# Layer 0 of a two-layer kernel rebuilt: two expert slots instead of three experts, one block, activation split on VectorE

## The reference

```python
xn = _layernorm(x, axis=-1)
s = _L0_attn_ref(xn, Wq, bq, Wk, bk, Wv, bv)      # per token: q, k, v of 16 x heads; 16 x 16 scores, softmax, mix
g = _silu(_L0_ffn_ref(xn, gate_w, gate_b, w1, b1, w2, b2))
x = x + s * g
...
# in _L0_ffn_ref
router_input = jnp.concatenate([h, modality_ratio], axis=-1)
gate_scores = jax.nn.softmax(router_input @ gate_w + gate_b, axis=-1)
top_val, top_idx = jax.lax.top_k(gate_scores, TOP_K)              # TOP_K = 2 of 3
top_val = top_val / (jnp.sum(top_val, axis=-1, keepdims=True) + 1e-08)
expert_out = _expert_outputs(h, w1, b1, w2, b2)                   # tanh, gelu, silu
for i in range(TOP_K):
    j = top_idx[:, 0, i]                                          # the expert of the batch's FIRST token
    moe_out = moe_out + top_val[..., i:i + 1] * expert_out[j, batch_idx]
```

## Time and profile before

| what | value |
|---|---|
| median of the runs | 1755.26 us |
| the profiled execution's own time | 1760.71 us |
| its span | 1759.0 us |
| TensorE busy | 1498.3 us (85%), mean granted clock 0.914 |
| VectorE busy | 1146.7 us (65%) |
| ScalarE busy | 604.9 us |
| GpSimd busy | 340.3 us |
| first product with an expert's matrix starts | 88.29 us |
| last operation of layer 0 on VectorE ends | 521.1 us |

### The profile page before, as it was taken

How to read it: one execution, slowest core, us unless ns; L and a number is a source line. 1 busy time by engine, 2 the same in 40 slices (tenths; PEclk the granted TensorE clock), 3 DMA queues, 4 the chain that set the end, 5 groups by cost and what they waited for, 6 DMA issues and landing times. The chain is left out here.

```text
span 1759.0 us, 21810 instructions
## 1 busy us (share of the span) xinstructions
PE 1498.3 (85%) x7034; PEld 1025.7 (58%) x7034; DVE 1146.7 (65%) x2429; ACT 604.9 (34%) x859; POOL 340.3 (19%) x382
## 2 busy tenths in 40 slices
PE   0399979898855884799999999599999999999969
PEld 0366757576634552577777777455555555555447
DVE  5575875858754544555555544388888888888427
ACT  4223233232312431011111111016666666666632
POOL 2243342433411320000000000002122221221211
PEclk9988988889876987799999999759999999999979
DMA  7200010100004433000000000221221211211032
GB/s 258 105 1 1 0 49 0 48 1 1 24 26 151 161 123 114 31 22 27 25 19 19 22 11 4 48 42 28 42 43 28 55 29 29 55 29 29 1 133 83
DMA packets 48600, 84.27 MB, mean 48 GB/s; under 512 B 8899, under 2 KB 16657, under 8 KB 48506
## 3 DMA queue, kind: packets, MB, share of 16 engines
q1 hardware_dynamic: 41874, 78.13, 15.1%
q10 hardware_dynamic: 6632, 4.97, 0.9%
HBM read 58.54 MB, written 24.26 MB: 47 GB/s over the span
## 5 line engine op out<-in xcount | busy, mean ns | idle before, releaser
L1502 ACT ACTIVATE f_prob<-f_bank 128x1024 f32<-128x1024 f32 (+3 forms) x384 | 302.1, 811 | 187.7 <-PE f_bank L1599 183.9
L1522 DVE CUSTOM_DVE_ANT_0 f_bank<-f_bank,f_mask 128x128 f32<-128x128 f32 (+3 forms) x512 | 247.7, 504 | 67.4 <-PE f_bank L1581 54.6
L1581 PE MATMUL f_bank<-f_kst,f_qst 96*128 96x512 f32 (+3 forms) x768 | 271.1, 398 | 14.3 <-DMA f_qst<-q_scr 12.2
L1581 PEld LDWEIGHTS f_bank<-f_kst,f_qst 96*128 96x128 f32 x768 | 148.3, 197 | 161.5 <-DVE f_mx L1522 58.0
L1599 PE MATMUL f_bank<-f_qst,f_kst 98*128 98x512 f32 (+3 forms) x768 | 210.3, 357 | 1.2 <-ACT f_prob L1502 1.2
L1470 POOL TENSOR_SCALAR_AFFINE_SELECT f_prob<-f_prob 128x256 f32<-128x256 f32 x256 | 103.9, 406 | 434.5 <-ACT f_prob L1502 430.9
L1525 DVE TENSOR_REDUCE f_mx_first<-f_bank 128x1 f32<-128x512 f32 x256 | 175.9, 687 | 5.9 <-PE f_bank L1581 4.3
L1617 PE MATMUL f_bank<-f_prob,f_vst 128*32 128x512 f32 (+3 forms) x1536 | 164.5, 500 | 1.0 <-ACT f_prob L1502 0.9
L37 PE MATMUL d_bank<-xtl,d_wgh 128*128 (+1 forms) x352 | 143.1, 407 | 8.8 <-DMA d_zz<-z_gu_scr 8.8
L1187 ACT ACTIVATE d_hs<-d_bank 128x512 f32<-128x512 f32 (+1 forms) x44 | 26.3, 598 | 348.5 <-PE d_bank L39 348.5
L1599 PEld LDWEIGHTS f_bank<-f_qst,f_kst 98*128 98x128 f32 x768 | 130.3, 192 | 19.8 <-ACT f_prob L1502 9.3
(11 more groups left out here) (225 smaller groups left out, 2759.5 us busy)
## 6 DMA issues: line engine op xcount, KB each, us to landing
f_qst<-q_scr SPq DMA_DIRECT2D x32, 384.0 KB, 6.2
q_scr<-c_qh SPq DMA_DIRECT2D x32, 256.0 KB
wst<-L_ffn_w SPq DMA_DIRECT2D x6, 1024.0 KB, 5.7
f_kst<-k_scr SPq DMA_DIRECT2D x32, 192.0 KB, 5.3
d_qw<-L_ffn_qweight_gu SPq DMA_DIRECT2D x40, 128.0 KB, 2.5
xall<-L_attn_x SPq DMA_DIRECT2D x2, 2048.0 KB, 16.5
xb<-L_attn_x SPq DMA_DIRECT2D x4, 1024.0 KB, 5.3
x_d<-xb SPq DMA_DIRECT2D x4, 1024.0 KB, 4.3
```

Source lines behind the costliest of these rows:

```text
L1502: act.activation(prob[:, c // 2 % 2, c % 2 * 2:c % 2 * 2 + 2, lo:], score_bank[c % 2][:, :, lo:], ACT.Exp, scale=D ** -0.5).then_inc(exp_d ...
L1522: dve.tensor_tensor_reduce(sc, sc, mask[:, CH - w:CH], 1.0, LEAST, ALU.add, ALU.max, mx[:, u, h % 2, h // 2, q:q + 1]).then_inc(spare_free, 1)
L1581: pe.matmul(spare[v][:, 0:w], qst[0:M_ROW, u, h // 2, q * P:q * P + P], kst[0:M_ROW, u, h % 2, at:at + w], start=True, stop=True).then_inc ...
```

## The change

- The inner block is gone. x comes in four pieces, three of them into buffers that the main loop uses (`xb`), and chunk 0 is turned and projected while the statistics of the later pieces are taken. The q, k, v weights and biases are read on other queues and the bias row is spread by a matmul.
- The router runs once for each batch; its result (`idx`) is read by SyncE into registers and chooses which expert matrices are fetched into two slots (`w1h`, `w1l`, `w2h`, `w2l` with SL = 2). Slot 0 is expert 0 or 2, slot 1 expert 0 or 1. The four matrices of batch 1 are fetched and split during chunks 0 to 2.
- A chunk has 8 steps instead of 12. `second_product` runs two steps behind `first_product`, not one.
- Since a slot's function is not known when the program is written, ScalarE computes two functions of a slice (tanh into `t0`, silu or gelu in place into the bank) with input and bias masked to zero for the one that isn't chosen; VectorE adds the two in the bank, copies the sum to `ah` and subtracts for `al`. The next first product into this bank waits for VectorE's `split_ready`.
- `moe` of slot 0 is written by ScalarE; the gate is one Silu on ScalarE and two operations on VectorE.
- The exit of the scores, `s_sb`, is a tensor_tensor; scores of tile t + 1 go ahead of the mix of tile t.

```diff
-        w1h, w1l = sb("w1h", [P, EXPERTS, KT, E], F32R), sb("w1l", [P, EXPERTS, KT, E], F32R)
+        SL, UB, WB, AB = 2, 3, 3, 3
+        NF = SL * KT
+        w1h, w1l = sb("w1h", [P, SL, KT, E], F32R), sb("w1l", [P, SL, KT, E], F32R)
...
+            def weights(n, which):
+                w = (w1, w2)[n % 2]
+                sp.dma_start(wst[:, n % WB], w[bass.ds(which, 1)].rearrange("e (k p) f -> p (e k) f", p=P)).then_inc(w_in[n % WB], 16)
+
+            sp.wait_ge(routed, 1)
+            first = [sp.value_load(idx[0:1, 0, s:s + 1], min_val=0, max_val=EXPERTS - 1) for s in range(SL)]
+            weights(0, first[0])
...
+            def functions(c, m):
+                g, b, s, n = c * NF + m, c // 2, m // KT, m % KT
+                act.wait_ge(f1_ps, g + 1)
+                if g >= 2:
+                    act.wait_ge(sum_ready, g - 1)
+                for i, f in enumerate((ACT.Tanh, (ACT.Silu, ACT.Gelu)[s])):
+                    to = (t0[:, m % 2], bank[:, 2 + m % 2])[i]
+                    mm = act.activation(to, bank[:, 2 + m % 2], f, bias=b1m[:, b, s, i, n:n + 1], scale=msk[:, b, s, i:i + 1])
+                mm.then_inc(act_ready, 1)
...
+            def first_slot(c):
+                act.wait_ge(f2_step, c * NF + KT)
+                act.wait_ge(coef_ready, c + 1)
+                for t in range(TPC):
+                    act.activation(moe[:, t], bank[:, 4 + t], ACT.Copy, scale=coef[:, t, 0:1]).then_inc(moe_first, 1)
...
+            def sum_functions(c, m):
+                dve.wait_ge(act_ready, c * NF + m + 1)
+                dve.tensor_tensor(bank[:, 2 + m % 2], bank[:, 2 + m % 2], t0[:, m % 2], ALU.add).then_inc(sum_ready, 1)
+
+            def low_part_a(c, m):
+                g = c * NF + m
+                if g >= AB:
+                    dve.wait_ge(f2_step, g - AB + 1)
+                dve.drain()
+                dve.tensor_copy(ah[:, g % AB], bank[:, 2 + m % 2])
+                dve.drain()
+                dve.tensor_tensor(al[:, g % AB], bank[:, 2 + m % 2], ah[:, g % AB].bitcast(F32), ALU.subtract).then_inc(split_ready, 1)
...
+                for m in range(NF):
+                    sum_functions(c, m)
+                    low_part_a(c, m)
+                    if m == NF - 1 and c + 1 < CHUNKS:
+                        low_part_x(c + 1, 0)
+                        low_part_x(c + 1, 1)
+                    if m == 0:
+                        gate_shift(c)
+                    if c > 0 and m < TPC:
+                        finish(c - 1, m)
+                    if m == 1:
+                        sums(c, 0)
+                    if m in (1, 3, 5):
+                        scores(c, (m + 1) // 2)
+                    if m in (2, 4, 6):
+                        mix(c, m // 2 - 1)
+                        sums(c, m // 2)
+                    if m == 3:
+                        gate(c)
+                    if c == 0 and m == 1:
+                        low_part_w1(2)
...
+                mix(c, TPC - 1)
+                if c + 1 < CHUNKS:
+                    low_part_x(c + 1, 2)
+                    low_part_x(c + 1, 3)
+                second_slot(c)
...
             def first_product(c, m):
-                e, n = m // KT, m % KT
-                if m >= 2:
-                    pe.wait_ge(act_ready, c * NF + m - 1)
+                g, s, n = c * NF + m, m // KT, m % KT
+                if n == 0 and c % 2 == 0:
+                    pe.wait_ge(w1_ready, SL * (c // 2) + s + 1)
+                if g >= 2:
+                    pe.wait_ge(split_ready, g - 1)
...
+            router(0)
+            pe.wait_ge(w3_lo, 1)
+            project(0)
+            router(1)
+            pe.wait_ge(masked, 3)
+            for c in range(CHUNKS):
+                if c > 0:
+                    project(c)
+                for m in range(NF):
+                    first_product(c, m)
+                    if m >= 2:
+                        second_product(c, m - 2)
```

More of the change, by code:

```diff
@@ L363, in body @@
+            scales(0)
+            scales(1)
+            pool.wait_ge(w3_hi, 1)
+            pool.tensor_tensor(w3l[:, :, :], w3f, w3h[:, :, :].bitcast(F32), ALU.subtract).then_inc(w3_lo, 1)
+            scales(2)
+            scales(3)
+            pool.wait_ge(lrow_ready, B)
+            scores(0, 0)
+            low_part_w2(1)
+            for c in range(CHUNKS):
+                if c > 0:
+                    scores(c, 0)
                 for t in range(TPC):
                     if t + 1 < TPC:
-                        scores(now, t + 1)
@@ L448, in scores, with projected @@
+            def projected(c, t):
+                i = c * TPC + t
+                dve.wait_ge(qkv_ps, i + 1)
+                dve.tensor_tensor(qkv[:, t], bank[:, t % 2, 0:QKV], bias_row[:, c // 2], ALU.add).then_inc(qkv_ready, 1)
             def scores(c, t):
@@ L518, in finish @@
[L518 to L525 removed]
+                dve.tensor_tensor(coef[:, :, :], coef[:, :, :], coef2[:, :, :], ALU.add).then_inc(coef_ready, 1)
@@ new lines, in _ @@
+            low_part_x(0, 0)
+            low_part_x(0, 1)
+            token_logits(0)
+            low_part_x(0, 2)
+            low_part_x(0, 3)
+            dve.wait_ge(row_ps, 1)
+            for b in range(B):
+                dve.tensor_copy(bias_row[:, b, 0:QB], bank[:, 4, 0:QB])
+            dve.wait_ge(small_in, 64)
+            route(0)
+            dve.tensor_tensor(em[:, :], ident[0:BR, 0:EXPERTS], ident[0:BR, 32:BR], ALU.add)
+            dve.tensor_copy(b2r[:, :], b2f[:, :])
+            dve.drain()
@@ new lines, in _ @@
+            dve.tensor_tensor(b2r[32:BR], b2f[32:BR], b2r[32:BR].bitcast(F32), ALU.subtract)
+            masks(0)
+            statistics(2)
+            projected(0, 0)
+            projected(0, 1)
+            statistics(3)
+            token_logits(1)
+            projected(0, 2)
+            projected(0, 3)
+            low_part_w1(0)
+            route(1)
+            masks(1)
+            for c in range(CHUNKS):
+                if c > 0:
+                    for t in range(3):
+                        projected(c, t)
+                scores(c, 0)
+                if c > 0:
+                    projected(c, 3)
@@ L541, in body @@
                 dve.drain()
-                gate(now)
                 for m in range(NF):
-                    e, t = m // KT, m // 3
-                    dve.wait_ge(act_ready, c * NF + m + 1)
-                    dve.tensor_tensor(al[:, m % 2], af[:, m % 2], ah[:, m % 2].bitcast(F32), ALU.subtract).then_inc(split_ready, 1)
-                    if m % KT == 0 and e > 0:
-                        gather(c, e - 1)
-                    if m < TPC and before is not None:
-                        finish(before, m)
-                    if m == NF - 1 and after is not None:
-                        low_part(after, 0)
-                        low_part(after, 1)
-                    (scores, sums, mix)[m % 3](c, t)
```

797 lines of the change are left out of this document (402 added, 395 removed).

## The result

The changed kernel took **1635.89 us** (median, 1633.67 to 1636.85), the kernel before beside it 1754.26 us: a ratio of 0.9316 (0.929 to 0.9342). Forecast: 1668 us, range 1630 to 1722. The direction and the range held; the gain was 118 us where 87 were forecast. The profiled execution took 1635.7 us, its span 1634.0 us, against 1760.7 and 1759.0 before. (That execution of the kernel before was one of its longer ones, so the profiles are 125 us apart and the medians 118.)

A forecast was written before the change was run, and what follows sets the result against it. VectorE was to become the bound (71 us a chunk, TensorE 60). Start 71, chunk 0 78.1, chunks 1 and 2 173.0, weights 18, chunk 3 94: 434 instead of 521, -87 us, so 1668 us, range 1630 to 1722.

The forecast's parts named there:

- Its sum for a middle chunk, 71 us: VectorE's operations in one middle chunk, added step by step, 71 us against TensorE's 60, making VectorE the bound.
- Two signs were missed: Signs in the loop that would show the forecast right: `sc` near 3.4 us mean and `s_sb` at 0.3.
- T: Zero point of a chunk: the last low part of x is there and projection starts; the next was put at 81.
- the chain by hand: One chunk followed through its engines: TensorE waits of 3.3 and 8.3 us, last low part at 77.1 us.
- TensorE stays the bound: Rival for the loop: the chunk shrinks with TensorE's work to 79 us, time 1634; chance 0.17.
- loop start: Part ahead of the loop, with routing and masks of both batches on the path: 71 us (63 to 80).
- makes first products 6 and 7 late by 5 us: In a chunk, a half-clock stretch behind TensorE's second wait delays these products by 5 us; next chunk starts at 81.
- for what a chain by hand leaves out ... I add 5: Allowance of 5 us a chunk for unlisted waits, since a middle chunk of before had 14.0 us; gives 86.5.
- The clock term: Two TensorE waits a chunk, each followed by a 13.6 us stretch at 0.50; one hidden, one costing 5 us.
- Weights: Splitting batch 1's weights inside chunks 0 to 2 adds 7, 4 and 7 us: 18, bounds 12 and 24.
- this rival: `s_sb` loses its 0.05 us race and is held by GpSimd's `pb`: 71 us in all, time 1739; chance 0.12.
- the last rival (slower): TensorE never returns to 2.4 GHz because every step waits: a chunk of 137 us, time 1876; chance 0.04.

The follow-up runs named there:

- e1: Changed kernel with GpSimd's next `pa` waiting until VectorE has written `sc`, not only until it has reduced `pa`: 1617.11 us.
- e3: Changed kernel without VectorE's addition of the two functions in the bank: 1617.19 us.
- e7: Changed kernel with GpSimd's `pa` waiting for `sc` and one of three matmuls (w1l times xth) left out of each first product: 1615.77 us.
- e8: Changed kernel with ScalarE, not VectorE, writing the high part `ah` out of the summed bank, and VectorE waiting for it: 1645.23 us.
- e11: Kernel before with the new split only: ScalarE makes the function once in the bank, VectorE makes high and low part from it: 1737.15 us, ratio 0.9868.
- e6: Changed kernel with the old split: ScalarE computes one function twice, VectorE only subtracts from SBUF, choice of function left out: 1640.09 us.
- e4: Kernel before with most of the third expert's matmuls left out and the other engines as they were: 1735.14 us, ratio 0.9848.
- e2: Changed kernel with one of the three matmuls of every first product (w1l times xth) left out: 1625.13 us.
- e5: Changed kernel without TensorE's wait for the masks of both batches ahead of the loop: 1627.31 us.
- e10: Changed kernel with `pa` waiting for `sc`, no TensorE wait for batch 1's masks, gate coefficients and GpSimd's w2 low part moved: 1592.81 us.

## Why the prediction was right, and 32 us too long

**Right.** VectorE becomes the bound (e1 and e3, and e7 against e1), as the order of its operations and not by its busy time (e8). Its sum for a middle chunk, 71 us, met 70.97 in chunk 1 by luck in part: in the 70.97 are 2.28 us of `w1l` and 1.95 us of a held `s_sb`, which the 71 hasn't got, so its own terms measured 66.7. It was added up from start to start, with the gaps. CAST out of a bank at 0.69 us: 0.692. No bank operation held. The stores of `x_d` at 181.9, 266.5 and 354.6 us are 85 and 88 us apart (forecast 82 to 93). Two signs were missed: `sc` 4.09 us in the mean (3.4), and `s_sb` held in two of sixteen. `al` is what TensorE waits for, near the places named (timeline of TensorE, chunk 1):

```profile
158.59 0.79 PE L37 MATMUL bank<-xtl,w1h 128*128 128x512 f32 x1 [3.65 <-DVE al L555]
...
193.38 0.80 PE L37 MATMUL bank<-xtl,w1h 128*128 128x512 f32 x1 [7.02 <-DVE al L555]
```

They end 17.9 and 52.7 us behind T = 140.66; the chain by hand had 3.3 us to T + 17.3 and 8.3 to T + 53.7, so here the mechanism was right in its detail. `route(1)` was held once ahead of the loop, by GpSimd's `w2l` (VectorE's timeline):

```profile
54.44 4.45 DVE L419 TENSOR_TENSOR abs_sum<-abs_sum,rstd 128x8 f32<-128x8 f32 x1
```

**The rival "TensorE stays the bound" gave 1634 us, 2 us from the result, and is still wrong.** Its chunk of 79 us and its mechanism (time goes with TensorE's work) are refuted by e7 against e1 (20.2 us less of TensorE's busy time for 1.3 to 4.2 us) beside e3, and not by the total. Its number met the right one by luck: VectorE's chain had a length near 80 as well.

**Too long, by term.** My end of layer 0 was 434, measured 396.0:

| term | forecast | measured | off |
|---|---|---|---|
| loop start | 71 | 66.1 | -5 |
| chunk 0, weights | 78.1 + 7 | 74.5 | -11 |
| chunk 1, weights | 86.5 + 4 | 80.0 | -11 |
| chunk 2, weights | 86.5 + 7 | 91.3 | -2 |
| chunk 3 | 94 | 84.0 | -10 |

- The terms that weren't there are "makes first products 6 and 7 late by 5 us", by which the next T went from 77.1 to 81, and "for what a chain by hand leaves out ... I add 5". (81 and 5 are 86; the prediction went on with 86.5.) The chain without both is 77.1 us. Chunk 1 took 80.0, and 80.0 less its 2.28 us of `w1l` and 1.95 us of held `s_sb` is 75.8. In chunk 3 the last `mix` ends 75.7 us behind T by the chain, and by the trace 387.85 - 312.00 = 75.9 us. The two terms enter four times: 4 x 9.4 = 38 us. The 5 us were read from the 14 us of waits of the old chunk, whose TensorE waited for others; the chain of this prediction follows those waits itself.
- The clock term: TensorE did fall to 1.2 GHz in both waits, as the windows behind them show.

```profile
158.59:161.50 2.91, 2.91 (x7) 2.33 (x8) 2.67 (x6) 0.72 (x3) 2.01 (x1) 0.50 0.00 0
193.38:199.00 5.62, 5.62 (x13) 4.00 (x13) 5.29 (x8) 1.89 (x4) 2.98 (x1) 0.50 0.01 4
```

  But TensorE worked at that clock for 2.9 and 5.6 us and not for 13.6 (of the 13.6 us of the earlier trace rows, 1.9 are before TensorE goes on at 230.38), and VectorE waited 0.2 us for ScalarE's functions in the whole chunk: nothing became late.
- Chunk 0 has no gate of a chunk before it: four `finish` of 1.4 us that I took off nowhere, 5.5 us.
- Weights: forecast 18 us, of which GpSimd's `w2l` between `pb` and `pa` 4.5 each. Measured: `sc` held for 7.4 us (chunk 0) and 7.3 us (chunk 2) more than by `pa` alone, three `w1l` of 2.28, and 1.95 us by which the `w2l` at the end of chunk 1 held `s_sb` (2.24 us at 217.30). That is 23.5 us, so this term was 5.5 too small.
- `s_sb`: of twelve races of 0.05 us (the fourth tile of a chunk has no `pb` behind it) one was lost, in chunk 2 (last section), so this rival came true by 5.6 us of its 71. It and the longer hold of `sc` make chunk 2 longer than chunk 1: 7.2 + 3.6 = 10.8 of 11.3 us, with the 1.95 us of chunk 1 taken off.
- The start: `route(0)` ran from 29.0 to 33.8 us, and not to 38.

Put together: 434 - 38 - 5 (start) - 5.5 + 5.5 + 5.6 = 396.6 us, measured 396.0. The terms that were too long, and those that were too short, are all found in the trace, and nothing large is left over.

**The parts of the change.** The start brought 22 us (66.1 against 88.3), by the trace. The loop brought 103. The new split alone is worth 23 us on the old blocks (e11); on the new ones, against the old split, 0 to 7 us (e6, which has no sum to make, so a kernel with the choice of functions would need more). The remainder of the loop's gain, some 80 us, comes with the blocks: four steps fewer, the second product two steps behind, the shorter gate and ScalarE's part of `moe`. No run takes these apart. Only for the four steps is there a hint: in e4, taking most of the third expert's matmuls alone brought 26 of 63 us, and the change leaves out those steps' `al`, functions and gather too.

The prediction set the Trainium skill, "TensorE: Matmul & The Clock Gate", section "HAM oscillation — how this bites in real kernels", beside its clock term. The trace agrees: behind the waits of 3.65 and 7.02 us in chunk 1 TensorE worked at a granted clock of 0.50. But between such stretches it came back each time, so the chunk's granted clock was 0.91, higher than the 0.86 of the middle chunk of before, and the last rival (slower) did not come true.

## What to carry to other kernels

Where VectorE and GpSimd work side by side, look first for VectorE operations whose duration doesn't fit their size (0.43 us shapes that take 4 or 12 us): let them read PSUM, or put them where GpSimd has nothing queued, and follow what GpSimd's next operation then meets. An engine at 87% may be waiting for another's order: take work from each in turn (e3, e4, e7 against e1) before the loop is called bound by it, and look in the profile at what the edit did to the others' busy time and to the clock (e2). Here a chain followed along the bounding engine was right within 1 to 2 us a chunk, and each of the two terms put on top of it was wrong.

## What the runs showed of the hardware

- VectorE's operation on two SBUF tiles did not always get its turn between two operations of GpSimd. At 83.86 us `sc` waited past two such borders (86.32 and 90.91) for 11.79 us; in e5 `w1l`, issued 0.28 us behind the start of GpSimd's `w2l`, ran at the next border, and so did a `w1l` of the kernel after (49.85 us, 4.67 us long) behind GpSimd's `pa`. What decides is open.
- Once in twelve `s_sb` came 0.44 us late and lost the race that it won otherwise (VectorE, then GpSimd, kernel after, chunk 2). In e1, e2, e3, e5, e7 and e10 the same `s_sb` of the same chunk is late by 0.44 us and held for 5.7 to 5.9 us, so it isn't chance; the cause of the 0.44 us is open.

```profile
295.47 2.28 DVE L506 TENSOR_REDUCE so<-pb 128x128 f32<-128x2048 f32 x1
298.19 5.87 DVE L508 TENSOR_TENSOR s_sb<-so,rsum 128x128 f32<-128x128 f32 x1 [0.44 <-issue]
```

```profile
297.89 6.02 POOL L216 TENSOR_TENSOR pb<-at,qkv 128x2048 f32<-128x2048 f32 x1 [4.79 <-DVE so L506]
```

  The Trainium skill, "SBUF — State Buffer", section "SBUF: two separate sides", has the two engines exclude each other for a whole instruction, whoever is first. These rows agree, with 5.87 us for an operation of 0.29.
- It works the other way round too: a held `w1l` (e5) made GpSimd's `pa` take 6.67 us instead of 4.47, and the `w1l` at 49.85 us in the kernel after made `w2l` take 6.54 instead of 4.6.
- The size of a held operation played no part in these two: four numbers took 4.39 us in e1, eight numbers 4.45 us at 54.44 us in the kernel after.
